# A second accumulation table for half of the expert pairs, read back midway, in a fused attention and mixture-of-experts kernel

## The chip, the cores and the metric

The kernel runs on one core of a Trainium2 chip. The metric is the device time of one execution in microseconds (us), as the median of several runs. The engines are named as the profile names them: PE (TensorE matmul, PEld its weight loads), DVE (VectorE), ACT (ScalarE), POOL (GpSimd) and SP (SyncE, which here only issues DMAs). A queue written SPq or POOLq is the engine's issuing of DMAs.

## The reference

The input x has 2 sequences of 1024 tokens with 256 values each, all float32. The block is

    x1  = layernorm(x + attention(x))
    out = layernorm(x1 + moe(x1))

- The attention has 16 heads of 128, RMS norm and rotary factors on queries and keys, scores capped by 50 * tanh(s / 50), a causal mask and softmax.
- The mixture of experts (MoE) routes each token to 6 of 32 experts, picked within 3 of 8 groups. Each expert takes its first 48 tokens at most. An expert computes silu(g) * u from one product (256 to 2 x 176) and a second product back to 256. Its rows are scaled by the token's weight and summed per token. A shared expert of 2 x 352 runs on every token and is added.

So behind the experts every token's row is a sum over up to six expert rows, and this sum is what the change touches.

## The kernel before

**Attention.** Eight pairs of heads, four steps each (two heads times two sequences) are run in a software pipeline: step s does the scores and softmax of its head while PE projects the queries and keys of step s+1. In each step the inverse RMS of the queries is written by SP to the table `rq_rows` in HBM in four small DMAs (line 344) and read back broadcast to all partitions into `rqB`, which is the tile `qsq` (line 346, function `rq_broadcast`). DVE scales the raw queries with it (line 1183) and splits them into a high and a low part, and then PE can compute scores.

**Start.** SP issues the first weights and x transposed, then x itself into `yacc` (line 337, semaphore `x_in`), in which the residual and the attention output add up. DVE waits for `x_in` right behind its splitting of x transposed, ahead of everything else of step 0. Then SP writes zeros from the tile `pacc` into the table `acc_rows` in nine DMAs (line 353) and into a strip of `x_rows` (line 354), and only then comes to the first `rq_broadcast`. POOL waits for the zeros before it starts step 0, as it will use `pacc` for the softmax sums from step 1 on.

**MoE.** After the routing POOL gathers the token rows of each pair of experts with an indirect DMA (`gather`, line 1054): 128 rows to a pair, 16 pairs. Four pairs form a group q with the semaphore `xg_in[q]`. PE turns the gathered rows (`slots_turned`, line 673, eight turns of a 128x512 tile, two to a group), DVE copies them to `xbT`. For pair p PE computes gate and up (`gate_up`, line 685), turns the activation (`turn_act`, line 696), and computes the down product (`expert_down`, line 706). The order of PE's work is written out by hand: gate_up(p+1), turn_act(p), then fillers, then expert_down(p). The fillers are the last piece of the shared expert's first product (`shared_up(11)`, line 594, dictionary `FILL_UP`) and twelve pieces of its second (`shared_down`, line 634, `FILL_DOWN`), which DVE adds into `yacc` (line 1436). `SLOT_TURNS` says behind which pairs the later groups are turned. Groups 0 and 1, eight gathered pairs, are turned before pair 0.

ACT scales the rows of a pair into one of four `ye` buffers (`expert_out`, line 907). POOL adds them to the rows of their tokens in `acc_rows` with an indirect DMA that accumulates (`scatter`, line 1060). The first expert of each pair has the upper half of `acc_rows` and the second the lower half, so that within one scatter no row is met twice; between scatters it may be, and so scatter p waits on POOL until scatter p-1 has landed (semaphore `added`). `expert_out(p)` waits until scatter p-4 has landed, as it reuses its buffer. Expert weights have eight buffers; SP loads those of pair p, 1.06 MB, as soon as the down product of pair p-8 is done (lines 383 and 384).

**End.** When all scatters have landed and PE has done the shared down products, SP reads `acc_rows` back into `accA` and `accB` (lines 401 and 402, sixteen DMAs). PE sums `yacc`, `accA` and `accB` in PSUM with identity matmuls (`add_rows`, line 638; the parts of `yacc` are done ahead), DVE takes the statistics, POOL the power, ACT normalises, and SP writes the output.

## Time and profile before

| | us |
|---|---|
| three runs | 1113.54, 1117.14, 1119.96 |
| median | 1117.14 |
| profiled execution | 1117.59 |
| its span, first to last instruction | 1115.9 |
| mean granted TensorE clock | 0.964 of full |

| engine | busy us | share of the span |
|---|---|---|
| PE | 1023.3 | 92% |
| PEld | 809.9 | 73% |
| DVE | 840.0 | 75% |
| ACT | 697.5 | 63% |
| POOL | 642.0 | 58% |

The busy shares are averages over stages with different limits: attention takes the first 900 us or so, routing and experts the rest. What bounds a stage is read from the chain that ended last and from the waits in that stage. The chain is followed back from the last instruction of the program, at each step to what released it. A DMA in it lasts from its issue to its landing. Granted clock 1.00 is 2.4 GHz for TensorE, 0.50 is 1.2 GHz.

### The profile page before, as it was taken

To read this page: it belongs to the slowest core of one execution; us is meant where nothing else is said; L and a number is where in the kernel's file an instruction comes from. 1 tells how busy PE (TensorE), PEld (TensorE's weight loads), DVE (VectorE), ACT (ScalarE), POOL (GpSimd) and SP (SyncE) were. 2 spreads that over 40 slices of the span, in tenths; PEclk is the share of its full clock that TensorE was granted. 3 is DMA by queue.
4 is the path that set the end of the run, shared out by engine and by line. 5 is a ranking of instruction groups with operands and counts; after the bars stand their busy time and mean duration, and the time that the engine had idled before them with its cause. 6 is when DMAs were issued, how large, how long until landed. Compare 5 with 4: busy or idle time off the path is not lost.

```text
span 1115.9 us, 17459 instructions
## 1 busy us (share of the span) xinstructions
PE 1023.3 (92%) x6048; PEld 809.9 (73%) x6048; DVE 840.0 (75%) x1376; ACT 697.5 (63%) x1159; POOL 642.0 (58%) x660
## 2 busy tenths in 40 slices
PE   4699999999999999999999999999999859889865
PEld 3478878887888788888878887888788746345432
DVE  3389898989898989888998889888988775613103
ACT  3377767777777777777777777777777723222212
POOL 0167666666676666666666666666667542353232
PEclk8899999999999999999999999999999978989888
DMA  9111011101100100010001000100000019539327
GB/s 337 46 39 33 24 36 40 33 30 39 30 20 29 39 30 20 30 39 29 20 29 39 30 20 29 40 29 20 20 20 20 20 30 289 129 101 253 74 29 231
DMA packets 47256, 66.77 MB, mean 60 GB/s; under 512 B 7904, under 2 KB 38592, under 8 KB 47168
## 3 DMA queue, kind: packets, MB, share of 16 engines
q1 hardware_dynamic: 43376, 60.65, 17.7%
q0 software_dynamic: 3072, 4.46, 2.3%
q8 instruction: 48, 0.79, 0.3%
q10 hardware_dynamic: 720, 0.54, 0.1%
q14 instruction: 40, 0.33, 0.1%
HBM read 54.35 MB, written 11.29 MB: 59 GB/s over the span
## 4 chain that ended last, share of the span: by engine, by line
PE 64%; DVE 14%; DMA 9%; issue 6%; POOL 3%; ACT 3%; SPq 1%; DVEq 0%; POOLq 0%; ACTq 0%
PE ps L417 19%; PE ps L418 18%; PE ps L419 17%; DMA acc_rows<-ye,acci 7%; DVE prob_lo L1098 7%; PE ps L451 5%; DVE qraw L1165 2%; PE ps L594 2%; POOL pacc L976 2%; PE ps L638 1%; DMA yacc<-in_x 1%; DVE qhat_lo L1098 1%; DVE qraw L1183 1%; DVE kT_lo L1098 1%; PE ps L604 1%
## 5 line engine op out<-in xcount | busy, mean ns | idle before, releaser
L1098 DVE TENSOR_TENSOR prob_lo<-praw,prob_hi 128x1024 fp32r<-128x1024 f32 (+7 forms) x256 | 304.6, 1213 | 1.7 <-ACT prob_hi L753 1.7
L959 POOL TENSOR_SCALAR_AFFINE_SELECT praw<-praw 128x128 f32<-128x128 f32 x256 | 120.7, 472 | 275.1 <-ACT praw L805 255.8
L976 POOL TENSOR_TENSOR pacc<-pacc,praw 128x768 f32<-128x768 f32 (+2 forms) x192 | 233.1, 1214 | 27.7
L799 ACT ACTIVATE praw<-ps,rk 128x1024 f32<-128x1024 f32 (+7 forms) x256 | 185.8, 740 | 64.3 <-PE ps L419 60.3
L753 ACT ACTIVATE prob_hi<-praw 128x1024 fp32r<-128x1024 f32 (+7 forms) x256 | 168.6, 685 | 1.3 <-POOL praw L959 1.3
L805 ACT ACTIVATE praw<-praw 128x1024 f32<-128x1024 f32 (+7 forms) x256 | 167.9, 683 | 0.0
L417 PE MATMUL ps<-qhat_hi,kT_hi 128*128 128x512 f32 (+3 forms) x384 | 135.1, 352 | 10.5 <-DVE qhat_lo L1098 10.1
L417 PE MATMUL ps<-prob_hi,vS_hi 128*128 128x512 f32 (+3 forms) x384 | 136.0, 354 | 6.0 <-DVE prob_lo L1098 6.0
L418 PE MATMUL ps<-prob_lo,vS_hi 128*128 128x512 f32 (+3 forms) x384 | 133.3, 347 | 0.0
L418 PE MATMUL ps<-qhat_lo,kT_hi 128*128 128x512 f32 (+3 forms) x384 | 133.0, 346 | 0.0
L419 PE MATMUL ps<-qhat_hi,kT_lo 128*128 128x512 f32 (+3 forms) x384 | 132.8, 346 | 0.0
L419 PE MATMUL ps<-prob_hi,vS_lo 128*128 128x512 f32 (+3 forms) x384 | 132.5, 345 | 0.0
L417 PE MATMUL ps<-xT_hi,wqk_hi 128*128 128x512 f32 x256 | 103.3, 404 | 23.8 <-DVE xT_lo L1098 11.9
L1210 DVE SCALAR_TENSOR_TENSOR yacc<-ps,rsum,yacc 128x256 f32<-128x256 f32 x256 | 111.5, 477 | 6.7 <-PE ps L419 5.8
L418 PE MATMUL ps<-xT_lo,wqk_hi 128*128 128x512 f32 x256 | 102.2, 399 | 0.0
L419 PE MATMUL ps<-xT_hi,wqk_lo 128*128 128x512 f32 x256 | 101.8, 397 | 0.0
L417 PEld LDWEIGHTS ps<-qhat_hi,kT_hi 128*128 128x128 f32 x384 | 72.8, 190 | 30.8 <-issue 12.8
L417 PEld LDWEIGHTS ps<-prob_hi,vS_hi 128*128 128x128 f32 x384 | 72.6, 189 | 17.6 <-DVE prob_lo L1098 12.1
L774 ACT ACTIVATE ksq<-ps 128x512 f32<-128x512 f32 x64 | 38.3, 599 | 65.8 <-PE ps L419 65.8
L419 PEld LDWEIGHTS ps<-qhat_hi,kT_lo 128*128 128x128 f32 x384 | 72.7, 189 | 8.4
L419 PEld LDWEIGHTS ps<-prob_hi,vS_lo 128*128 128x128 f32 x384 | 72.4, 189 | 8.2
L418 PEld LDWEIGHTS ps<-qhat_lo,kT_hi 128*128 128x128 f32 x384 | 73.0, 190 | 6.0
(161 smaller groups left out, 2255.6 us busy)
## 6 DMA issues: line engine op xcount, KB each, us to landing
qsq<-rq_rows SPq DMA_DIRECT2D x32, 512.0 KB, 4.0
wgu<-in_wgu SPq DMA_DIRECT2D x16, 704.0 KB
wd<-in_wd SPq DMA_DIRECT2D x16, 352.0 KB
wraw<-in_wqkv SPq DMA_DIRECT2D x16, 256.0 KB, 4.5
acc_rows<-pacc SPq DMA_DIRECT2D x8, 512.0 KB, 10.5
wvraw<-in_wqkv SPq DMA_DIRECT2D x16, 128.0 KB, 2.7
woraw<-in_wo SPq DMA_DIRECT2D x16, 128.0 KB, 4.1
yacc<-in_x SPq DMA_DIRECT2D x1, 2048.0 KB, 13.8
```

Source lines behind the costliest of these rows:

```text
L417: mm(out_, left[0], right[0], start=start, stop=False)
L418: mm(out_, left[0], right[1], start=False, stop=False)
L419: return mm(out_, left[1], right[0], start=False, stop=stop)
L451: last = mm(ps[32 * g:32 * g + 32, bank_no, c0:c0 + 32 * TT].rearrange("p (j r) -> p j r", r=32), ones[:, :], by_strip[:, g], start=True, ...
L753: return nc.scalar.activation(dst, src, ACT.Copy)
L774: nc.scalar.activation(ksq[:, cols], bank, ACT.Square).then_inc(ksq_done, 1)
L799: nc.scalar.activation(praw[:, raw_at(b, j)], buf[:, P * j:T], ACT.Tanh, scale=rk[:, b, j:j + 1]).then_inc(tanh_done, 1)
L805: nc.scalar.activation(tile, tile, ACT.Exp, scale=CAP).then_inc(exp_done, 1)
L959: nc.gpsimd.affine_select(out=diag, in_=diag, compare_op=ALU.is_ge, fill=0.0, base=0, pattern=[[1, P]], channel_multiplier=-1).then_inc(ma ...
L976: nc.gpsimd.tensor_tensor(pacc[:, P * j:T], before, raw, ALU.add).then_inc(pacc_done, 1)
L1098: v.tensor_tensor(dst, x_, hi.bitcast(F32), ALU.subtract).then_inc(done, 1)
L1210: last = v.scalar_tensor_tensor(y, ps[:, bank_no, D * i:D * i + D], rsum[:, k, 2 * u + i:2 * u + i + 1], y, ALU.mult, ALU.add)
```

## The change

- A second table, `acc2_rows`, of the size of `acc_rows`. Pairs 1, 3, 5 and 7 scatter into it (`SIDE`), the other twelve into `acc_rows` (`MAIN`). Each table has its own semaphore, and a scatter waits only for the one before it on its own table.
- When the four side scatters have landed, SP reads `acc2_rows` back in eight DMAs of 512 KB into `accA`, the last four of them each after an add that frees its place. DVE adds them to `yacc` in eight additions of 128x1024, two each behind pairs 11, 12, 14 and 15 (`SIDE_ADDS`). SP waits for all eight before it reads `acc_rows` as before, and PE before it sums `yacc`.
- Both tables are zeroed. The zero writes stand behind the first `rq_broadcast` on SP, and POOL waits for them ahead of step 1, no more ahead of step 0.
- DVE waits for x ahead of step 1.
- Only group 0 is turned before pair 0. Groups 1, 2 and 3 are turned behind pairs 1, 4 and 7, where groups 2 and 3 were behind pairs 2 and 5. The last `shared_up` moves from pair 0 to pair 1, the first `shared_down` from pair 1 to pair 0. Gathers 10 to 15 are issued two at a time behind scatters 0, 1 and 2.

```diff
-FILL_UP = {0: 11}
-FILL_DOWN = {p: p - 1 for p in range(1, 13)}
+FILL_UP = {1: 11}
+FILL_DOWN = {0: 0} | {p: p - 1 for p in range(2, 13)}
-SLOT_TURNS = {2: 2, 5: 3}
+SLOT_TURNS = {1: 1, 4: 2, 7: 3}
+SIDE = [p for p in range(WR) if p % 2]
+MAIN = [p for p in range(PAIRS) if p not in SIDE]
+SIDE_ADDS = {11: (0, 1), 12: (2, 3), 14: (4, 5), 15: (6, 7)}
...
+        def written(engine, p):
+            if p in SIDE:
+                engine.wait_ge(side_added, 16 * (SIDE.index(p) + 1))
+            else:
+                engine.wait_ge(added, 16 * (MAIN.index(p) + 1))
...
+            rq_broadcast(0, 0)
             sp.wait_ge(zeros_set, 1)
             zero = pacc[:, :]
-            rows = acc_d.rearrange("(p r) d -> p (r d)", p=P)
-            for c0 in range(0, 2 * ACCR // P * D, T):
+            for table in (acc_d, acc2_d):
+                rows = table.rearrange("(p r) d -> p (r d)", p=P)
+                for c0 in range(0, 2 * ACCR // P * D, T):
...
-            rq_broadcast(0, 0)
...
-            sp.wait_ge(added, 16 * PAIRS)
+            sp.wait_ge(side_added, 16 * len(SIDE))
+            sp.wait_ge(gu_read, SHARED_UNITS)
+            for n in range(8):
+                if n >= 4:
+                    sp.wait_ge(side_done, n - 3)
+                four = slice(4 * (n % 4), 4 * (n % 4) + 4)
+                sp.dma_start(accA[:, four, :], side_v[n // 4][:, four, :]).then_inc(side_in[n], 16)
+            sp.wait_ge(side_done, 8)
+            sp.wait_ge(added, 16 * len(MAIN))
             sp.wait_ge(sd_done, NT)
...
+                if n == SHARED_FOURTH:
+                    pe.wait_ge(sd_added, 1)
...
-                if i == 0:
+                if i == 1:
                     pe.wait_ge(gu_read, SHARED_UNITS)
...
-                if n >= 2:
-                    pe.wait_ge(xbt_read, n - 1 if n < 2 * KC else n)
+                if n >= KC:
+                    pe.wait_ge(xbt_read, n)
...
-            for n in range(2 * KC):
+            for n in range(KC):
                 slots_turned(n)
             gate_up(0)
...
             pe.wait_ge(sd_added, ADDED)
+            pe.wait_ge(side_done, 8)
...
                 if p >= 4:
-                    act.wait_ge(added, 16 * (p - 3))
+                    written(act, p - 4)
...
-            pool.wait_ge(zeros_out, 16 * ((2 * ACCR // P * D + T - 1) // T + 1))
-            for q in range(STEPS):
+            step(Step(0, 0, "first"))
+            pool.wait_ge(zeros_out, 16 * (2 * ((2 * ACCR // P * D + T - 1) // T) + 1))
+            for q in range(1, STEPS):
                 step(Step(0, q, "first"))
...
             def scatter(p):
                 pool.wait_ge(ey_evac, p + 1)
-                if p:
-                    pool.wait_ge(added, 16 * p)
-                nc.gpsimd.indirect_dma_start(acc_d, bass.IndirectOffsetOnAxis(ap=acci[:, p:p + 1], axis=0), ye[:, p % 4, :], None,
-                                             compute_op=ALU.add).then_inc(added, 16)
+                row = bass.IndirectOffsetOnAxis(ap=acci[:, p:p + 1], axis=0)
+                if p in SIDE:
+                    if SIDE.index(p):
+                        pool.wait_ge(side_added, 16 * SIDE.index(p))
+                    nc.gpsimd.indirect_dma_start(acc2_d, row, ye[:, p % 4, :], None, compute_op=ALU.add).then_inc(side_added, 16)
+                else:
+                    if MAIN.index(p):
+                        pool.wait_ge(added, 16 * MAIN.index(p))
+                    nc.gpsimd.indirect_dma_start(acc_d, row, ye[:, p % 4, :], None, compute_op=ALU.add).then_inc(added, 16)
...
-            for p in range(8, 12):
+            late = list(range(8, PAIRS))
+            for p in late[0:2]:
                 gather(p)
             for p in range(PAIRS):
-                if p in FILL_UP:
-                    shared_product(FILL_UP[p])
                 scatter(p)
                 if p == 1:
-                    for g in range(12, PAIRS):
-                        gather(g)
+                    shared_product(FILL_UP[p])
+                for g in late[2 * p + 2:2 * p + 4]:
+                    gather(g)
...
             split_x(1)
-            dve.wait_ge(x_in, 16)
...
-            for q in range(STEPS):
+            step(Step(0, 0, "first"))
+            rows_in()
+            for q in range(1, STEPS):
                 step(Step(0, q, "first"))
...
+            def add_side(n, shared):
+
+                dve.wait_ge(side_in[n], 16)
+                dve.wait_ge(sd_added, shared)
+                if n >= 4:
+                    dve.wait_ge(side_done, n - 3)
+                four = slice(4 * (n % 4), 4 * (n % 4) + 4)
+                v.tensor_tensor(yacc[:, four, :], yacc[:, four, :], accA[:, four, :], ALU.add).then_inc(side_done, 1)
...
-            for n in range(2 * KC):
+            for n in range(KC):
                 slots_turned(n)
...
                 if p in FILL_DOWN:
                     add_shared(FILL_DOWN[p])
+                for n in SIDE_ADDS.get(p, ()):
+                    add_side(n, min(p, ADDED))
```

## Rows read from the trace of the kernel before

**Rows 1.** Page of the profile: the chain that ended last, shares of the span by line.

```profile
PE ps L417 19%; PE ps L418 18%; PE ps L419 17%; DMA acc_rows<-ye,acci 7%; DVE prob_lo L1098 7%; PE ps L451 5%; DVE qraw L1165 2%; PE ps L594 2%; POOL pacc L976 2%; PE ps L638 1%; DMA yacc<-in_x 1%; DVE qhat_lo L1098 1%; DVE qraw L1183 1%; DVE kT_lo L1098 1%; PE ps L604 1%
```

**Rows 2.** Chain of waits, 0 to 70 us: start us, duration us, engine or DMA and line.

```profile
5.78 13.78 DMA yacc<-in_x
19.59 0.70 DVE qraw L1165
...
34.17 3.77 DMA qsq<-rq_rows
...
61.73 1.20 DVE qraw L1183
```

**Rows 3.** Timelines of DVE and PE, start: us, duration, operation [idle before it <- what ended it].

```profile
14.97 2.29 DVE L1098 TENSOR_TENSOR xT_lo<-praw,xT_hi 128x2048 fp32r<-128x2048 f32 x1 [0.38 <-ACT xT_hi L753]
...
20.33 0.79 PE L417 MATMUL ps<-xT_hi,wqk_hi 128*128 128x512 f32 x1 [3.78 <-DVE qraw L1165]
```

**Rows 4.** Timeline, SP queue, 0 to 140 us.

```profile
6.34 11.43 SPq L353 DMA_DIRECT2D acc_rows<-pacc  x9
...
54.34 1.30 SPq L344 DMA_DIRECT2D rq_rows<-sqT  x4
```

**Rows 5.** Windows: PE, PEld, DVE, ACT, POOL busy (count), then PEclk, DMA share, GB/s.

```profile
20.00:25.00 5.00, 4.67 (x11) 3.70 (x12) 1.39 (x3) 1.09 (x2) 0.00 (x0) 0.50 1.03 419
1020.00:1025.00 5.00, 4.59 (x30) 2.86 (x32) 2.13 (x5) 0.32 (x1) 0.00 (x0) 1.00 1.00 243
```

**Rows 6.** Timeline, PE, 957 to 1040 us.

```profile
980.52 1.04 PE L673 MATMUL ps<-ident,xg 128*128 128x128 f32 x8
986.69 1.97 PE L673 MATMUL ps<-ident,xg 128*128 128x128 f32 x8 [5.13 <-DMA xg<-x_rows,toki]
988.59 4.12 PE L685 MATMUL ps<-wgu,xbT 128*64 128x352 f32 x16
...
992.89 3.60 PE L594 MATMUL ps<-x1T,wsgu 128*96 128x512 f32 x8
...
997.33 1.36 PE L685 MATMUL ps<-wgu,xbT 128*64 128x352 f32 x8
...
1001.18 1.36 PE L685 MATMUL ps<-wgu,xbT 128*64 128x352 f32 x8
...
1006.57 0.66 PE L673 MATMUL ps<-ident,xg 128*128 128x128 f32 x4 [0.78 <-DVE xbT L1419]
```

**Rows 7.** Chain of waits, 860 to 1116 us.

```profile
1006.65 8.49 DMA acc_rows<-ye,acci
...
1025.76 9.13 DMA acc_rows<-ye,acci
...
1046.65 3.80 DMA acc_rows<-ye,acci
...
1087.25 3.87 DMA acc_rows<-ye,acci
...
1091.55 3.03 DMA accB<-acc_rows
```

**Rows 8.** Timeline, POOL, 910 to 1116 us.

```profile
986.21 0.98 POOL L1054 DMA_INDIRECT xg<-x_rows,toki  x1 [0.16 <-issue]
...
1008.52 1.01 POOL L1054 DMA_INDIRECT xg<-x_rows,toki  x1 [0.30 <-issue]
```

**Rows 9.** DMA issues, 1005 to 1016 us: what, queue, count, median us to landing.

```profile
xg<-x_rows,toki POOLq DMA_INDIRECT x4, 6.3
```

**Rows 10.** Timeline, PE, 1040 to 1116 us.

```profile
1061.24 0.42 PE L696 MATMUL ps<-ident,actE 128*88 128x128 f32 x2 [1.37 <-DVE actE L1425]
...
1065.74 0.66 PE L696 MATMUL ps<-ident,actE 128*88 128x128 f32 x2 [2.48 <-DVE actE L1425]
...
1068.81 3.78 PE L638 MATMUL ps<-yacc,ident 128*128 128x512 f32 x4
...
1094.62 2.07 PE L638 MATMUL ps<-accA,ident 128*128 128x512 f32 x2 [11.10 <-DMA accB<-acc_rows]
```

More of the change, by code:

```diff
@@ L139, in block_kernel @@
     acc_d = nc.dram_tensor("acc_rows", (2 * ACCR, D), F32, kind="Internal").ap()
+    acc2_d = nc.dram_tensor("acc2_rows", (2 * ACCR, D), F32, kind="Internal").ap()
     ctx = ExitStack()
@@ L301, in block_kernel @@
         et_done, et_read = sem("et_done"), sem("et_read")
-        ey_done, ey_evac, added = sem("ey_done"), sem("ey_evac"), sem("added")
+        ey_done, ey_evac, added, side_added = sem("ey_done"), sem("ey_evac"), sem("added"), sem("side_added")
+        side_in, side_done = [sem(f"side_in{n}") for n in range(8)], sem("side_done")
         acc_in = [sem(f"acc_in{k}") for k in range(NT // 2)]
         sum_done, var2, rln2, nmr_done, norm_done, out_done = sem("sum_done"), sem("var2"), sem("rln2"), sem("nmr_done"), sem("norm_done"), sem("out_done")
+        def written(engine, p):
[3 more added lines that the diff above has]
+                engine.wait_ge(added, 16 * (MAIN.index(p) + 1))
         def sum_place(i):
@@ L316, in block_kernel @@
         accB_v = acc_d[ACCR:ACCR + N, :].rearrange("(i p) d -> p i d", p=P)
+        side_v = [acc2_d[ACCR * u:ACCR * u + N, :].rearrange("(i p) d -> p i d", p=P) for u in range(2)]
         out_v = out.rearrange("(i p) d -> p i d", p=P)
@@ L346, in rq_broadcast @@
                 sp.dma_start(rqB[:, :], rq_d[b:b + 1, :].to_broadcast([P, T])).then_inc(rqB_in, 16)
+            rq_broadcast(0, 0)
             sp.wait_ge(zeros_set, 1)
             zero = pacc[:, :]
-            rows = acc_d.rearrange("(p r) d -> p (r d)", p=P)
-            for c0 in range(0, 2 * ACCR // P * D, T):
-                cn = min(T, 2 * ACCR // P * D - c0)
-                sp.dma_start(rows[:, c0:c0 + cn], zero[:, 0:cn]).then_inc(zeros_out, 16)
+            for table in (acc_d, acc2_d):
+                rows = table.rearrange("(p r) d -> p (r d)", p=P)
+                for c0 in range(0, 2 * ACCR // P * D, T):
+                    cn = min(T, 2 * ACCR // P * D - c0)
+                    sp.dma_start(rows[:, c0:c0 + cn], zero[:, 0:cn]).then_inc(zeros_out, 16)
             sp.dma_start(x1_d[N:ACCR, :], zero[:, 0:XD]).then_inc(zeros_out, 16)
-            rq_broadcast(0, 0)
             next_wqkv = wqkv_d[2:H].rearrange("(n e) p m c d -> n e p m c d", e=2)
@@ L669, in slots_turned @@
                     pe.wait_ge(xg_in[q], 16 * 4)
-                if n >= 2:
-                    pe.wait_ge(xbt_read, n - 1 if n < 2 * KC else n)
+                if n >= KC:
+                    pe.wait_ge(xbt_read, n)
                 for r in range(4):
-                    last = nc.tensor.transpose(ps[:, n % 2 if n < 2 * KC else 1, P * r:P * r + P], xg[:, 4 * q + r, P * c:P * c + P], ident[:, :])
+                    last = nc.tensor.transpose(ps[:, n % 2 if n < KC else 1, P * r:P * r + P], xg[:, 4 * q + r, P * c:P * c + P], ident[:, :])
                 last.then_inc(xbt_done, 1)
@@ L691, in turn_act @@
                 if p == 0:
-                    pe.wait_ge(xbt_read, 2 * KC)
+                    pe.wait_ge(xbt_read, KC)
                 else:
@@ L1202, in tile, with rows_in @@
                 lo_of(prob[1][:, AT[j]:AT[j] + n], praw[:, raw_at(b, j)], prob[0][:, AT[j]:AT[j] + n], plo_done)
+            def rows_in():
+                dve.wait_ge(x_in, 16)
             def out_projected(b, k, u, step, count, bank_no):
@@ L1418, in slots_turned @@
                 dve.wait_ge(xbt_done, n + 1)
-                v.tensor_copy(xbT[:, c, 512 * q:512 * q + 512], ps[:, n % 2 if n < 2 * KC else 1, :]).then_inc(xbt_read, 1)
+                v.tensor_copy(xbT[:, c, 512 * q:512 * q + 512], ps[:, n % 2 if n < KC else 1, :]).then_inc(xbt_read, 1)
             def product(p):
```

## The prediction, made before the changed kernel was run

> **What bounds the kernel now.** I read the page first, then the chain of waits at both ends, then the timelines of the engines in those stretches. The change touches the first step of the attention and everything behind the routing; the 900 us between keep their work, so what is gained or lost at the start is only carried through them. The page gives the scatter-adds into `acc_rows` 7% of the chain that ended last [rows 1]. The chain of waits shows how: from 1006.65 to 1091.1 it is one scatter-add after another, because each waits on POOL for the one before to land. While expert weights are loading one takes 8.5 to 9.1 us, with idle DMA engines 3.8 to 3.9; from the one at 1046.65 to the last at 1087.25 are nine steps of 4.51, so 0.7 us lie between a landing and the next start [rows 7]. PE could go faster: a pair costs it 3.85 us (997.33 to 1001.18) [rows 6], and at 1083.5 it has done all its other work and idles 11.1 us for the rows read back [rows 10]. From pair 1 on the scatter chain sets the time.
>
> Two waits ahead of that chain matter. The first pair can't start until eight gathers have landed: PE idles 5.13 us, turns the second four tiles in 1.97, and then needs 4.12 us for the sixteen gate-and-up matmuls of two pairs, where eight take 1.36 later [rows 6]. And at the start DVE stands from 17.26 (14.97 + 2.29 [rows 3]) to 19.59 for the load of x into `yacc` [rows 2], which nothing needs before step 1; PE idles 3.78 us meanwhile [rows 3] and comes back at the lower of its two clocks (granted 0.50, 1.2 GHz, from 20 to 25 us [rows 5]).
>
> **Part 1, the start.** The wait for x leaves step 0. DVE copies the first queries at 17.3 instead of 19.6: 2.3 us. PE then pauses 1.5 us instead of 3.8. The two key projections behind it are 12 matmuls, before at half clock (11 in 4.67 us [rows 5]); at full clock they would end 2.4 us earlier. That the clock holds is an estimate from the pair stage: after a pause of 1.37 us two small matmuls took 0.42 us, after one of 2.48 us they took 0.66 [rows 10]. Together the chain to the first `rq` broadcast comes 4.7 us earlier; bounds 2.3 and 4.9.
>
> The zero writes move behind that broadcast and double: nineteen DMAs, 9.06 MB, from about 29.9 (34.17 + 0.4 less 4.7 [rows 2]). At the 419 GB/s of [rows 5] they take 21.6 us, to 51.5. The DMA engines were free then. POOL's wait for them stands before the first use of `pacc` in step 1, which comes near the end of step 0, where DVE scales the next queries at 61.73 [rows 2], now 57.0: hidden by some 5 us. But SP's queue is full when the second `rq` broadcast comes. Its source was ready at 54.3 [rows 4], now at 49.6; its small writes get behind the zeros' tail and 0.26 MB of `wvraw` and land near 53.5, and the broadcast itself, 3.8 us [rows 2], near 57.5, where DVE wants it at 57.0. I charge 0.7 us, between 0 (the small writes slip through) and 5 (the zeros go at 0.33 MB/us). SP's issuing is no limit: nine zero DMAs took 11.43 us to issue with other loads ahead [rows 4]. Net of part 1: **-4.0 us**, with ends -4.9 and +1.
>
> **Part 2, the first pair.** PE turns tiles 0 and 1 by 981.56 (980.52 + 1.04 [rows 6]); DVE's copy keeps it some 0.9 us, as the 0.78 at 1006.57, and at 982.45 pair 0 may start. Gone are the rest of the wait for the gathers, the second turning and, as the pause is short, the half clock: two products in 2.4 instead of 4.1. The last shared product (3.60 busy, 3.43 until the next can start [rows 6]) moves to pair 1, and a shared down product takes its place; one of these and the down product are what is left of a pair's 3.85 after 1.2 for gate-and-up and 0.35 for the turn: 2.3 together. So 982.45 + 2.4 + 0.35 + 2.3 = 987.5 for the end of pair 0, where it was 997.4: 9.9 us earlier. POOL's gather 8 was issued at 986.21, and 8 and 9 with 1.3 each end at 988.8 [rows 8], just clear for scatter 0. Pair 1 takes 1.2 + 0.35 + 3.43 + 1.0 = 6.0 us and ends at 993.5; the two turnings with the copy between cost 2.0, so pair 2 ends at 999.4, then 3.85 each with 2.0 more behind pairs 4 and 7: 1003.2, 1007.1, 1012.9, 1016.8, 1020.6 and 1026.5 (pair 8). The other gathers are out behind scatter 2 and late for nothing.
>
> **Part 3, the side table.** Scatters 0, 2, 4, 6 and 8 to 15 are one chain, 1, 3, 5, 7 another; POOL issues both in order. Behind a pair's end I put 1.6 us for ACT's two copies and the issue. Under load a scatter's step is 9.1 + 0.7 = 9.8 us, and two may now fly at once. Even: 0 at 989, 2 at 1001, 4 at 1011, 6 at 1020.5. Odd: 1 at 995, 3 at 1005, 5 at 1015, 7 at 1024.5, landing before 1030 as the loads stop. These, eight of 1.06 MB at the 243 GB/s of [rows 5], start 10 us earlier too and are over near 1026. How much two in flight slow each other no row shows directly. The nearest: the scatter of 1006.65 took 8.49 us though four gathers followed it on the same queue from 1008.52 on [rows 7, 8], no longer than the 9.13 at 1025.76 with nothing behind it, and these gathers, in flight together, landed 6.3 us after their issue each [rows 9]. So I take no slowdown; the other end is that they take turns.
>
> By the Trainium skill (DMA: Bandwidth & Descriptors, Queues, rings and completion order) each DMA engine goes round between its queues and drains a packet of one before it changes to the next. Both scatters stand in the one queue of POOL, so while SP's loads keep theirs full the second would win no share of its own. By that rule the sum would be that of rival A.
>
> Scatter 8 waits for 6 alone and issues when its rows are ready, at 1028.3. Before it was issued at 1055.6 (1087.25 less seven steps of 4.52 [rows 7]): 27.3 us later. The readback gives part of it back. When scatter 7 has landed SP reads both side halves, 4.2 MB; at 0.33 MB/us (between the 419 and the 243 GB/s of [rows 5]) that loads the DMA engines for 12.7 us between 1030 and 1047. Scatters 8 to 10 then need 5.6 to 7.5 us instead of 3.8: I charge 8, between 0 and 12 (two and a half at the loaded price). The last lands at 1091.1 - 27.3 + 8 = 1071.8: **-19 us** for parts 2 and 3.
>
> The eight adds of 128x1024 cost DVE some 1.15 us each (half of the 2.29 for 128x2048 in [rows 3]), 9 us in all, behind pairs 11, 12, 14 and 15. DVE comes to pair 11 near 1037, after the first side rows are in (1033), and has added all by 1054; what stands behind them, the turn of pair 12, is 7 us ahead of its scatter. PE's sums now also wait for the adds: they ran from 1068.81 to 1083.5 [rows 10] and now run from 1054 to 1069, still ahead of 1071.8, cover of 3 us. ACT only reads another semaphore. Behind the last scatter all is as before, 24.8 us to the end of the span, the accumulated rows read back in 3.0 us [rows 7] and PE cold as before.
>
> **Sum.** The profiled execution took 1117.59 us, its span 1115.9, so 1.7 lie around it; it stands 0.45 above the median of 1117.14. 1117.6 - 4 - 19 = 1094.6, against the median 0.4 less: **about 1094.3 us**.
>
> **Rivals.**
> *A, two scatters in flight take turns.* If under load each doubles the other's time, the first eight last until 1040, the readback runs from 1042 to 1056, and the last lands near 1081: 9.5 us gained in place of 19, total 1104. For it: the loaded price is itself a time in queues. Against it: the gathers beside the scatter of 1006.65. Chance 0.2.
> *B, the zeros block the start.* They run at the 243 GB/s of the weight loads, 37 us, to 67; the second `rq` broadcast lands near 72, 15 us behind its need. Part 1 becomes +10, total 1108.5. Against it: the 419 GB/s of [rows 5] were largely these writes. Chance 0.05.
> *C, slower: the side readback becomes the end.* From the last side scatter to the last add lie four loads, four more that wait for adds, and the work of pairs 14 and 15, some 24 us; then PE's 15 us of sums, which must end before SP may read `acc_rows`. To be 5.6 us slower than before SP must start at 1100.7 (1091.1 + 4 + 5.6), so scatter 7 would have to land after 1061, 32 us behind my date. With steps of 17 us in both chains that happens: total 1123 or more. No row asks such a price. Chance 0.02.
> *D, little comes through:* loads, readback and adds eat what the two chains give, 1111.6 to 1122.7. Chance 0.03.
>
> **Numbers.** Forecast 0.7, A 0.2, B 0.05, C 0.02, D 0.03. About 0.5%, 5.6 us, is what a measurement can tell from no change: faster 0.95, same 0.03, slower 0.02. The forecast's own bounds are 1087 (start -4.9, readback 3 instead of 8, scatters at 7 us under load) and 1100 (start 0, readback 10); the range goes on to A: 1087 to 1105.
>
> **What would show it.** DVE's first `qraw` copy near 17.3 and PEclk at 1.0 between 18 and 22; the zeros between 30 and 52, the broadcast of step 1 landing near 57; pair 0's down product 10 us earlier behind the turning of tile 0; side scatters overlapping main ones at 9 us each, not 18; scatter 8 some 27 us earlier, scatter 15 some 19. I am wrong if a loaded scatter with a partner takes over 12 us, if DVE idles at the first side add, or if PE's sums end after the last scatter lands.

## The result, and the profile after

The changed kernel takes 1101.19 us (median of 4 runs, 1099.12 to 1103.33), the kernel before beside it 1117.33 (1113.54 to 1119.96): a ratio of 0.9863, 95% interval 0.9836 to 0.9889, so 16 us less where 23 were forecast. The profiled execution took 1103.33 us, its span 1101.6 where it was 1115.9.

The pair stage first: the chain of waits of the changed kernel from 985 us on (start us, duration us, what), where [rows 7] stood.

```profile
1033.65 3.82 DMA acc_rows<-ye,acci
...
1038.20 7.41 DMA acc_rows<-ye,acci
...
1046.34 4.25 DMA acc_rows<-ye,acci
...
1056.20 5.82 DMA acc_rows<-ye,acci
...
1071.84 3.87 DMA acc_rows<-ye,acci
...
1079.32 16.47 PE ps L661 x32
```

Scatter 8 at 1033.65 is the first link; ahead of it the chain is PE's pairs, no scatter. Of the eight scatters in the chain four take the quiet 3.8 us (two of them are left out here); the four from 1038.20 to 1056.20 take more (the one left out among them, of 1051.32, took 4.15). The timeline of PE, where [rows 6] stood:

```profile
985.63 1.04 PE L696 MATMUL ps<-ident,xg 128*128 128x128 f32 x8
987.66 2.59 PE L708 MATMUL ps<-wgu,xbT 128*64 128x352 f32 x16 [0.99 <-DVE xbT L1453]
...
991.83 1.08 PE L729 MATMUL ps<-wd,actT 88*64 88x256 f32 x8
```

PE waits 0.99 us for DVE's copy in place of the gathers, and pair 0's down product ends 7.3 us behind the turning of tile 0. The scatters 0 to 7, main and side, by tile, issued between 985 and 1032 us:

```profile
L1091 POOL DMA_INDIRECT acc_rows<-ye,acci x4: 1560/1611/1638, 994.2 to 1023.8; - x4
L1087 POOL DMA_INDIRECT acc_rows<-ye,acci x4: 1557/1592/1623, 1000.2 to 1028.4; - x4
...
DMA to landing us min/median/max: 6.5/7.1/7.7
```

L1087 is the side table, L1091 the main one. Eight scatters start in 34 us. Each is in flight together with the next for 0.4 to 4.2 us; the one issued at 1010.69 had a partner for 6.7 of its 7.4 us. None lands later than 7.7 us after its issue; one at a time they took 8.5 to 9.1 [rows 7].

So the stage did what it was meant to. From the turning of tile 0 to the last landing it took 1091.12 - 980.52 = 110.6 us and takes 1075.71 - 985.63 = 90.1: **20.5 us less** (forecast 19). But tile 0 is turned at 985.63 in place of 980.52: the stage starts **5.1 us later**, where 4.0 earlier was forecast. That came from the start. SP's queue, 28 to 90 us, where [rows 4] stood:

```profile
30.18 0.35 SPq L358 DMA_DIRECT2D qsq<-rq_rows  x1
30.57 21.16 SPq L367 DMA_DIRECT2D acc_rows<-pacc  x18
...
55.09 1.35 SPq L356 DMA_DIRECT2D rq_rows<-sqT  x4
57.65 0.34 SPq L358 DMA_DIRECT2D qsq<-rq_rows  x1
...
86.14 1.30 SPq L356 DMA_DIRECT2D rq_rows<-sqT  x4
```

The last row is the writes of the third broadcast, which in the kernel before were these:

```profile
82.31 1.30 SPq L344 DMA_DIRECT2D rq_rows<-sqT  x4
```

The first `rq` broadcast is issued at 30.18 (34.17 before [rows 2]): the 4 us are there. Then SP spends 21.16 us on issuing eighteen zero DMAs, 1.2 us each. That is about as long as one takes to move (0.52 MB at 418 GB/s is 1.25 us), so SP is held back, and the second broadcast goes out at 57.65. The zeros are also in flight longer than SP is issuing them: those issued from 48 us on land 5.0 to 6.3 us after their issue, so the last ones behind 55 us. What the DMA engines moved, in slices of 1 us from 25 to 65 us:

```profile
GB/s 0 0 0 1 3 0 152 233 332 410 434 410 426 418 418 430 410 426 404 424 406 410 422 426 414 422 414 418 420 383 264 132 13 57 283 270 365 82 0 0
```

DVE at 14 to 25 us and at 60 to 70 us:

```profile
17.46 1.28 DVE L1194 COPY qraw<-ps 128x512 f32<-128x512 f32 x2
...
61.68 2.21 DVE L1212 SCALAR_TENSOR_TENSOR qraw<-qraw,gcur,qsq 128x1024 f32<-128x1024 f32 x1 [3.10 <-DMA qsq<-rq_rows]
63.92 2.18 DVE L1138 CAST qhat_hi<-qraw 128x1024 fp32r<-128x1024 f32 x1
66.14 2.44 DVE L1128 TENSOR_TENSOR qhat_lo<-qraw,qhat_hi 128x1024 fp32r<-128x1024 f32 x1
```

The first copy came at 17.46 (19.59 before). At 61.68 DVE has waited 3.10 us, and its three operations take 6.8 us where the same three at 34.63 took 1.28, 0.69 and 1.22. The POOL timeline beside them:

```profile
60.70 2.11 POOL L1000 TENSOR_TENSOR pacc<-praw 128x896 f32<-128x896 f32 x1 [0.15 <-POOL pacc L996]
62.95 9.38 POOL L1000 TENSOR_TENSOR pacc<-pacc,praw 128x768 f32<-128x768 f32 x6
```

POOL is adding up `pacc` all that time. The whole balance: +5.1 at the start of the stage, -20.5 in it, and +1.1 behind it (PE's last sums took 16.47 us, 15.44 before): 14.3 us, which are the spans' 1115.9 - 1101.6. The +1.1 is not shown to come from the change: in the two versions of the kernel before that follow below the same sums took 16.03 and 15.86 us.

Of the 5.1 us, 3.8 are there at the third `rq` broadcast, whose writes SP issues at 86.14 us where it was 82.31, and are carried through the attention. The other 1.3 I put down to PE's clock: from 935 to 945 us it was granted 0.50, the 1.2 GHz level (the PEclk column of the windows, as in [rows 5]), where it had 0.71 and 0.95 before. At the start, from 15 to 25 us, it was at full speed. Changed kernel:

```profile
15.00:25.00 10.00, 7.21 (x45) 4.96 (x43) 5.56 (x7) 4.07 (x8) 0.00 (x0) 1.00 0.33 104
...
935.00:940.00 5.00, 5.00 (x25) 5.00 (x25) 0.00 (x0) 3.99 (x6) 0.08 (x1) 0.50 0.98 257
940.00:945.00 5.00, 5.00 (x18) 4.03 (x19) 1.39 (x3) 0.00 (x0) 1.18 (x1) 0.50 0.97 310
```

and before:

```profile
935.00:940.00 5.00, 5.00 (x23) 3.15 (x23) 2.68 (x19) 1.30 (x3) 1.27 (x1) 0.71 0.97 269
940.00:945.00 5.00, 5.00 (x12) 2.02 (x11) 4.85 (x36) 2.37 (x3) 1.26 (x1) 0.95 1.04 264
```

From the third broadcast's writes to the turning of tile 0 it is 899.5 us here and 898.2 before. Of the versions below with the same start, the one that also had 0.50 from 935 to 945 us (the two-table run) took 899.6, the others, at higher clocks, 897.7 to 898.5. So a difference of one or two microseconds between two profiles need not be the edit's.

### The profile page after: what moved, and what is told of

Its sections match the earlier page's. It is cut to its first block, busy times and chain, and to the rows that moved or that the text cites. A ratio compares the mean times of both kernels' runs of the same rounds, so it can differ in the third digit from the quotient of the medians.

```text
span 1101.6 us, 17494 instructions
## 1 busy us (share of the span) xinstructions
PE 1019.9 (93%) x6048; PEld 810.3 (74%) x6048; DVE 848.3 (77%) x1384; ACT 698.1 (63%) x1159; POOL 643.0 (58%) x660
## 3 DMA queue, kind: packets, MB, share of 16 engines
q0 software_dynamic: 3072, 4.46, 2.2%
## 4 chain that ended last, share of the span: by engine, by line
PE 69%; DVE 15%; issue 5%; DMA 5%; SPq 2%; POOL 2%; ACT 2%; DVEq 0%; ACTq 0%; POOLq 0%
PE ps L438 19%; PE ps L439 18%; PE ps L440 18%; DVE prob_lo L1128 6%; PE ps L472 5%; DMA acc_rows<-ye,acci 3%; PE ps L617 3%; SPq L367 2%; DVE qraw L1194 2%; POOL pacc L1000 2%; PE ps L661 1%; PE ps L708 1%; DVE qraw L1212 1%; DVE kT_lo L1128 1%; PE ps L657 1%
## 5 line engine op out<-in xcount | busy, mean ns | idle before, releaser
L798 ACT ACTIVATE ksq<-ps 128x512 f32<-128x512 f32 x64 | 38.4, 599 | 60.6 <-PE ps L440 60.6
```

Source lines behind the costliest of these rows:

```text
L798: nc.scalar.activation(ksq[:, cols], bank, ACT.Square).then_inc(ksq_done, 1)
```

## The experiments

**The start alone.** The kernel before with part 1 of the change; once with one table's zeros, once with both.

```diff
 e1_start_one_table and e2_start_two_tables, against the kernel before
+            rq_broadcast(0, 0)
             sp.wait_ge(zeros_set, 1)
 (e2)        for table in (acc_d, acc2_d):
...
-            rq_broadcast(0, 0)
...
-            dve.wait_ge(x_in, 16)
...
-            for q in range(STEPS):
+            step(Step(0, 0, "first"))
+            dve.wait_ge(x_in, 16)
+            for q in range(1, STEPS):
```

> The kernel before with part 1 of the change alone and one table: x is waited for behind step 0, the first rq broadcast stands ahead of the zeros, POOL waits for the zeros behind step 0, but only the nine zero DMAs of acc_rows and the strip are written. Theory Q (SP stands at a full queue: in the changed kernel eighteen zero DMAs are issued 1.2 us apart from 30.6 on, so SP is free for the second broadcast only at 55.1 and not at 51.2): nine are issued by about 42, the second broadcast goes out on time, DVE scales the queries of step 1 at about 58.5 instead of 61.7, and the time is 3 to 4 us below before: 1113.5. Rival X (moving the wait for x or the order on SP costs by itself, whatever the number of zeros): as slow as with two tables, 1119 to 1121.

> The same as the run with one table, but both tables are zeroed, so part 1 of the change in full and nothing of the rest; the second table is not used. Theory Q: the second broadcast lands at 61.7, 3 us late, DVE's three operations behind it run into POOL's additions into pacc and take 6.8 us instead of 3.2, and everything behind is 3.8 us later than before: 1121, so 7 us above the run with one table. Rival X: the same time as the run with one table. If the sum of parts holds, this run less 20 us is the changed kernel.

Measured: one table 1112.65 us (ratio 0.9965, 0.9946 to 0.9984), two tables 1119.29 (1.0036, 1.002 to 1.0053), the kernel before 1116.06. Both are within 2 us of theory Q, and rival X falls. The second table's zeros alone cost 6.6 us and turn the gain of the start into a loss. SP's queue and DVE with one table:

```profile
29.63 9.69 SPq L354 DMA_DIRECT2D acc_rows<-pacc  x9
...
56.71 1.28 DVE L1183 SCALAR_TENSOR_TENSOR qraw<-qraw,gcur,qsq 128x1024 f32<-128x1024 f32 x1
```

and with two:

```profile
30.27 21.17 SPq L357 DMA_DIRECT2D acc_rows<-pacc  x18
...
61.38 2.47 DVE L1186 SCALAR_TENSOR_TENSOR qraw<-qraw,gcur,qsq 128x1024 f32<-128x1024 f32 x1 [2.83 <-DMA qsq<-rq_rows]
```

Nine zero DMAs take 1.08 us each to issue as well, but are over before the second `rq` broadcast is ready (its writes go out at 49.39); eighteen are not. The rows with two tables are the changed kernel's over again: the start's loss needs nothing of the pair stage. What these two runs don't separate is whether the broadcast's writes are late because SP can't issue them or because they stand in its queue behind zeros that are still moving at 55 us; with more zeros both come together.

**The collision at 61 us.** The changed kernel, in which POOL holds step 1's first `pacc` work until DVE has made `qhat_lo`.

```diff
 e4_pool_held
+                    if st.first and st.q == 1:
+                        pool.wait_ge(qlo_done, 2)
```

> The changed kernel with one wait more: in step 1 POOL starts its additions into pacc only when DVE has split the queries of step 1. Theory P (the second half of the loss is that the late scaling and splitting, 2.21, 2.18 and 2.44 us instead of 1.28, 0.69 and 1.22, run beside POOL's additions and hold each other up at SBUF): the three take 3.2 us again, scores of step 1 start 3.6 us earlier, and of this 2 to 3.6 us stay, as POOL's additions end about as late as before the change: 1098.5. Rival Z (they were slow for another reason, such as the DMA just landing): the three stay at 6.8 us and the time is the changed kernel's or worse.

Measured: 1099.13 us (0.9853, 0.9822 to 0.9884), 2.1 us below the changed kernel; the intervals of the two ratios overlap, so the trace must say it. DVE, and POOL behind it:

```profile
60.55 1.28 DVE L1214 SCALAR_TENSOR_TENSOR qraw<-qraw,gcur,qsq 128x1024 f32<-128x1024 f32 x1 [3.64 <-DMA qsq<-rq_rows]
61.88 0.69 DVE L1140 CAST qhat_hi<-qraw 128x1024 fp32r<-128x1024 f32 x1
62.60 1.23 DVE L1130 TENSOR_TENSOR qhat_lo<-qraw,qhat_hi 128x1024 fp32r<-128x1024 f32 x1
...
64.03 0.29 POOL L996 COPY pacc<-praw 128x128 f32<-128x128 f32 x1 [5.39 <-DVE qhat_lo L1130]
```

The wait for the broadcast stays (3.64), the three operations are back at 3.2 us. So the wait comes with the zeros, and the slow DVE is POOL's additions beside it. Tile 0 is turned at 978.30, 7.3 us earlier than in the changed kernel; of these the third broadcast shows 5.9 (80.21 against 86.14), of which 1.0 was there at the first one (29.21 against 30.18), ahead of anything that the edit touches. The rest goes with PE's clock, granted 0.66 and 1.00 from 935 to 945 us and not 0.50. But the pair stage took 94.6 us in place of 90.1, and ate most of it: see below.

**Zeros that hold nobody.** The changed kernel with a zero tile of its own; after the first `rq` broadcasts each step's broadcast is followed by one zero DMA, and POOL waits for the zeros only before its scatters.

```diff
 e3_spread
+        zsrc = sb("zsrc", [P, 256])
...
+            def zeros_piece():
+                if pieces:
+                    dst, src = pieces.pop(0)
+                    sp.dma_start(dst, src).then_inc(zeros_out, 16)
...
-            pool.wait_ge(zeros_out, 16 * (2 * ((2 * ACCR // P * D + T - 1) // T) + 1))
...
+            pool.wait_ge(zeros_out, 16 * ZERO_PIECES)
```

> The changed kernel with the zeros taken from a 128x256 tile of their own and written one DMA at a time behind each of the following rq broadcasts, eighteen zero DMAs and two for the strip over the first five pairs of heads; POOL waits for them only ahead of the gathers. Theory Q: start as with one table, -3.5 us against before instead of +3.8, so 7 us below the changed kernel: 1094. Rival Y (what was lost at the start was lost to DMA bandwidth or to the longer table as such, and 512 KB of zeros a step disturb the broadcasts anyway): within 2 us of the changed kernel, 1099 to 1102.

Measured: 1097.11 us (0.983, 0.9796 to 0.9863), and 1097.15 (0.9841, 0.981 to 0.9873) when it was run once more beside the gated versions below. That lies between theory Q (1094) and rival Y (1099 to 1102). The start did more than theory Q asked: the writes of the second `rq` broadcast go out at 49.27, those of the third at 77.22, 5.1 us ahead of the kernel before, each zero DMA takes 0.44 us to issue, and DVE takes 1.28 us at 56.59. Tile 0 is turned at 976.71, 8.9 us before the changed kernel's. Only 4.1 of them arrive in the medians, too few for the intervals of the two ratios to part: the pair stage takes 94.7 us here too (94.5 in the second profile, whose two slow issues take 2.24 and 4.46 us). The timelines of POOL and DVE in it:

```profile
1038.63 2.44 POOL L1105 DMA_INDIRECT acc_rows<-ye,acci  x1 [6.36 <-DMA acc_rows<-ye,acci]
1046.41 4.37 POOL L1105 DMA_INDIRECT acc_rows<-ye,acci  x1 [5.34 <-DMA acc_rows<-ye,acci]
...
1038.41 2.36 DVE L1489 TENSOR_TENSOR yacc<-yacc,accA 128x1024 f32<-128x1024 f32 x2
1044.39 2.35 DVE L1489 TENSOR_TENSOR yacc<-yacc,accA 128x1024 f32<-128x1024 f32 x2
1047.00 2.35 DVE L1489 TENSOR_TENSOR yacc<-yacc,accA 128x1024 f32<-128x1024 f32 x2
```

Two scatters are issued in 2.44 and 4.37 us in place of 1.56, and both stand beside DVE's additions of the side rows. In the changed kernel the scatter of 1056.20 took 3.50 us to issue beside the additions of 1055.92, and the one of 1046.34 was issued 1.0 us ahead of the additions of 1047.33 and escaped. Counted from the turning of tile 0, the additions of pair 12 stand at +61.7 in both kernels and scatter 10 at +60.7 there, +61.9 here: a shift of 1.2 us decides.

The second run of this version (1093.95 to 1104.49 us in six executions) shows what the clock alone can do. Its profile is of the slowest execution, 1104.49 us. Its third broadcast goes out 0.3 us later than in the first profile, but its tile 0 is turned 6.1 us later, at 982.78: from 930 to 945 us PE was granted 0.50 there and 1.00 in the first. The same matmuls, first profile and second:

```profile
928.81 3.66 PE L642 MATMUL ps<-gwT,x1T 128*128 128x32 f32 x32
932.86 6.88 PE L642 MATMUL ps<-gwT,x1T 128*128 128x32 f32 x32
```

**A gate for DVE's additions.** The spread version, in which POOL counts its scatters and DVE's additions behind pairs 11, 12, 14 and 15 wait for scatters 9, 10, 11 and 12.

```diff
 e8_gated, against e3_spread
+ADD_BEHIND = {11: 9, 12: 10, 14: 11, 15: 12}
...
+                pool.sem_inc(issued, 1)
...
+                if p in ADD_BEHIND:
+                    dve.wait_ge(issued, ADD_BEHIND[p] + 1)
```

> The version with the spread zeros, and VectorE's side adds of pairs 11, 12, 14 and 15 now start only behind the issue of scatter 9, 10, 11 and 12. Theory (an add of 128x1024 on VectorE keeps GpSimd from issuing the scatter beside it: 1.56 us became 2.4 and 4.4 in the spread version): every scatter is issued in some 1.6 us, the stage from the turn of tile 0 to the last landing takes 90 to 91 us instead of 94.7, the time is 1097.1 - 4 = 1093. Rival (the adds don't hold the issues, or what they cost comes back as TensorE's sums, which wait for the last add): within 1.5 us of the spread version, 1095.6 to 1098.6.

> The spread version once more on the chip of the gated ones, for the difference: 1097 again, within 1.5 us.

Measured: 1093.62 us (1092.13 to 1094.57; 0.9806, 0.9779 to 0.9832) against 1097.15 of the spread version beside it, 3.5 us less, with intervals that overlap. The stage took 90.8 us. POOL's timeline, and DVE's additions behind pairs 12, 14 and 15:

```profile
1036.58 1.56 POOL L1107 DMA_INDIRECT acc_rows<-ye,acci  x1 [6.34 <-DMA acc_rows<-ye,acci]
1042.41 1.56 POOL L1107 DMA_INDIRECT acc_rows<-ye,acci  x1 [4.28 <-DMA acc_rows<-ye,acci]
1046.85 2.49 POOL L1107 DMA_INDIRECT acc_rows<-ye,acci  x1 [2.87 <-DMA acc_rows<-ye,acci]
...
1037.68 2.36 DVE L1492 TENSOR_TENSOR yacc<-yacc,accA 128x1024 f32<-128x1024 f32 x2
1043.67 2.35 DVE L1492 TENSOR_TENSOR yacc<-yacc,accA 128x1024 f32<-128x1024 f32 x2
1046.67 2.36 DVE L1492 TENSOR_TENSOR yacc<-yacc,accA 128x1024 f32<-128x1024 f32 x2 [0.33 <-POOLq L1108]
```

Scatters 10 and 11 are issued in 1.56 us and follow at 5.83 and 4.44 (7.78 and 7.63 in the spread version); scatter 12 is now hit instead. But the gate is not what spared 10 and 11. Only the additions of 1046.67 waited for POOL. Those of pair 12 stand at +61.7 behind the turning of tile 0, where they stood without the gate; it is scatter 10 that comes at +60.6 and not at +61.9. The reason lies ahead of every gated addition: scatter 8 landed after 3.97 us and not 5.24. So scatters 10 and 11 start 1.1 and 1.3 us ahead of the additions and escape, as scatter 10 did in the changed kernel. Where the gate did act it leaked: POOL's counter moves 0.2 us ahead of the scatter behind which it stands in the program, so DVE's additions start with the scatter.

Of the stage's 3.9 us 1.3 are scatter 8's landing, and 2.6 follow from it (step by step 1.95 and 3.19 gained, 2.53 given back at scatter 12). So the theory's time and stage came out, but the trace doesn't show them as the gate's work, and what the gate is worth stays open. The rival's first half, that the additions don't hold the issues, falls all the same. In the profiles of this document eleven issues of scatters 10 to 13 took 2.05 to 4.53 us, all beside such additions; in those without additions (before, one table, two tables, and the two below without a readback) none of these took over 1.56. And the gate, where it acted, put the additions 0.2 us ahead of a scatter, once here and twice in the last run below: 2.49 us each time. This version also beats the changed kernel, by 7.6 us in the medians and 6.4 by the ratios, whose intervals just don't meet (0.9832 and 0.9836 are their nearest ends).

**The side table alone.** The changed kernel with all sixteen scatters in one table, no readback and no additions (the second table is still zeroed).

```diff
 e5_no_side
-SIDE = [p for p in range(WR) if p % 2]
+SIDE = []
...
-SIDE_ADDS = {11: (0, 1), 12: (2, 3), 14: (4, 5), 15: (6, 7)}
+SIDE_ADDS = {}
...
-            sp.wait_ge(side_added, 16 * len(SIDE))
...
-                sp.dma_start(accA[:, four, :], side_v[n // 4][:, four, :]).then_inc(side_in[n], 16)
...
-            pe.wait_ge(side_done, 8)
```

> The changed kernel without the side table's use: all sixteen scatters in one chain on acc_rows, no readback midway, no adds, everything else as changed (the second table is still zeroed). Theory S (in the changed kernel PE sets the pace up to scatter 8, as two chains keep up with it; with one chain of 7.5 to 9 us steps under load the scatters fall behind PE by pair 4): the last scatter lands 95 to 98 us behind the turning of tile 0, where it is 90.1 with the side table, so 1107, and the side table is worth some 6 us, the earlier first pair 13 to 15. Rival A of the prediction (two in flight take turns, so one chain is as good): within 1.5 us of the changed kernel or faster, as the readback and the adds are gone.

Measured: 1108.96 us (0.9943, 0.9923 to 0.9964), stage 98.5 us, and rival A falls. The side table is worth 1109.0 - 1101.2 = 7.8 us, its readback already paid. In the chain of waits scatter 5 is still slow, and the first quiet scatter is the seventh, scatter 6:

```profile
1030.71 5.05 DMA acc_rows<-ye,acci
...
1036.49 3.79 DMA acc_rows<-ye,acci
```

**The first pair alone.** The changed kernel with the side table, but the first pair, its turnings and gathers as before.

```diff
 e7_turns8
-SLOT_TURNS = {1: 1, 4: 2, 7: 3}
+SLOT_TURNS = {2: 2, 5: 3}
...
-            for n in range(KC):
+            for n in range(2 * KC):
                 slots_turned(n)
...
```

> The changed kernel with the pair stage's order of before: two groups of gathered rows turned ahead of pair 0, the last shared product in pair 0, gathers as before; the side table stays. Theory S (PE sets the pace up to scatter 8): pair 0 ends 10 us later, pair 1 has 2.1 us less to do and one turning less stands between, so scatter 8 goes out some 6 us later and the time is 1107. Rival (the scatter chains set it throughout and have slack for a late start): 1102 or less.

Measured: 1111.74 us (0.9937, 0.9914 to 0.996), 4.7 above what was expected; stage 100.8. So the new first pair is worth 1111.7 - 1101.2 = 10.5 us. PE:

```profile
990.03 1.97 PE L694 MATMUL ps<-ident,xg 128*128 128x128 f32 x8 [5.11 <-DMA xg<-x_rows,toki]
```

The wait for the gathers is back. Taken out singly, the two parts lengthen the stage by 8.4 and 10.7 us, together 19.1 of the 20.5 that it gained: nearly additive, where the two forecast times, 1107 each, had put only 6 us on either.

**The readback's price.** The changed kernel with the side table written, but neither read back nor added: the output lacks the contributions of pairs 1, 3, 5 and 7.

```diff
 e6_no_readback
-SIDE_ADDS = {11: (0, 1), 12: (2, 3), 14: (4, 5), 15: (6, 7)}
+SIDE_ADDS = {}
...
-                sp.dma_start(accA[:, four, :], side_v[n // 4][:, four, :]).then_inc(side_in[n], 16)
...
-            pe.wait_ge(side_done, 8)
```

> The changed kernel with the side table written but neither read back nor added, so the output lacks the rows of pairs 1, 3, 5 and 7. My term for the readback was 8 us. The trace of the changed kernel has scatter 9 at 7.41 us, 10 at 4.25, 11 at 4.15 and 12 at 5.82, where the quiet ones take 3.8: 6.4 us in all. Theory R (all of that is the readback's DMAs and, for scatter 12, a DVE add that holds POOL's issue, 3.50 us instead of 1.56): all are at 3.8, 1095. Rival (the rest of the weight loads slows them): scatter 9 stays above 6 us and the time falls by 3 us or less.

Measured: 1096.27 us (0.9816, 0.9787 to 0.9845), 4.9 below the changed kernel (the intervals overlap a little), and the stage is 4.9 shorter, 85.1 us. Scatters 8 and 9:

```profile
1031.45 4.95 DMA acc_rows<-ye,acci
...
1037.14 3.66 DMA acc_rows<-ye,acci
```

From scatter 9 on all are near the quiet price, with 4.37 us for scatter 12 as the highest. Scatter 8 took 4.95 us here, 1.1 more than in the changed kernel, so the 4.9 us are rather too low for the readback and the additions.

**One more pair on the side.** As the gated version, with pair 9 in the side table and the additions behind pairs 12 to 15.

```diff
 e9_side_of_five, against e8_gated
-SIDE = [p for p in range(WR) if p % 2]
-ADD_BEHIND = {11: 9, 12: 10, 14: 11, 15: 12}
+SIDE = [1, 3, 5, 7, 9]
+ADD_BEHIND = {12: 10, 13: 11, 14: 12, 15: 13}
```

> As the gated version, with pair 9's scatter on the side chain too (five side, eleven main), so that the main chain has one step of some 4.5 us less, while the side readback starts one scatter later. Theory (the main chain sets the end all the way): pair 9 and pair 8 may fly together, the last landing comes 2 to 4 us earlier, time 1091 (2 below the gated version). Rival (from there TensorE's sums, which wait for the last side add, or the readback beside later scatters set the end): same as the gated version within 1 us, or slower by up to 3, and TensorE then has no idle time ahead of its last turns.

Measured: 1092.57 us (1089.98 to 1094.94; 0.9795, 0.9767 to 0.9824), 1.1 below the gated version: not to be told from it. The last scatter lands 90.0 us behind the turning of tile 0, 0.8 earlier than in the gated version, where the theory had 2 to 4. POOL and PE show why there is no more:

```profile
1031.99 1.56 POOL L1107 DMA_INDIRECT acc_rows<-ye,acci  x1 [2.29 <-ACT ye L948]
...
1046.66 2.49 POOL L1107 DMA_INDIRECT acc_rows<-ye,acci  x1 [4.61 <-ACT ye L948]
1052.08 2.49 POOL L1107 DMA_INDIRECT acc_rows<-ye,acci  x1 [2.93 <-DMA acc_rows<-ye,acci]
...
1069.93 1.13 PE L678 MATMUL ps<-accA,ident 128*128 128x512 f32 x2 [0.54 <-DMA accB<-acc_rows]
```

Scatter 10, issued at 1031.99 as SP begins the readback at 1031.96, lands only after 7.8 us, and the leaking gate lets DVE's additions start with scatters 12 and 13. PE idles 0.54 us ahead of its last sums, where it idled 6.59 in the gated version, and it is still the rows read back that it waits for: its own sums, which the rival named, are not the bound yet, but 0.5 us away from it. What the rows show is the rival's other half, the readback beside later scatters.

## Why the prediction was right and wrong

The time fell in the range and the sign was right; 6.9 us too much was promised. The profiled execution, 2.1 us slower than the median, misses by more, 8.7 us: 7.8 at the third broadcast (part 1), 1.3 behind it with the clock, 1.1 in the tail, less 1.5 that the pair stage gained over its forecast. So nearly all of it is part 1.

**Part 1, the steps that failed: "SP's issuing is no limit" and the zeros' end at 51.5.** The first was read from nine DMAs issued in 11.43 us with loads ahead [rows 4]. That row was itself the limit: 1.27 us each, where SP issues an unhindered DMA in 0.35 to 0.5. Eighteen of them take 21.16. The prediction knew that the queue would be full and that the broadcast's writes would stand behind the zeros' tail, and had them land near 53.5. But SP issued the last zeros at 51.78, and the DMA engines were at their full rate until about 55: the rate was as forecast, but it was reached only at 34 us (233 GB/s from 32 to 33 us), and 0.5 MB of the first broadcast moved with the zeros. The writes' source was ready at 51.2; they were *issued* at 55.09. So its 57.5 for the landing became 61.66, and a wait of 0.5 us one of 3.10. How much of the 4 us an SP that is never held would have saved, with the zeros still moving, no run shows. The term behind it was not in the sum at all: DVE's three operations then fell beside POOL's additions, 3.6 us. Charged were 0.7 us; against the forecast -4.0 the third broadcast stood at +3.8, a miss of 7.8. The two-table run shows a loss of 3.2 us in the time with nothing of the pair stage changed, the one-table run the gain of 3.4 that this part has without the second table; there the third broadcast's writes came 5.0 us earlier (forecast without the charge 4.7).

The rest of part 1 held: first copy at 17.46 (17.3), PE at full clock, granted 1.00 from 15 to 25 us, first broadcast 4.0 us earlier (4.7). The range's end for part 1, +1, was too near. Rival B, that the zeros block the start, priced the case at +10 with a slower transfer rate as its cause; the rate was as forecast (418 GB/s from 34 to 51 us).

**Part 2** held: PE's pause 0.99 (0.9), pair 0's down product 7.3 us behind the turning of tile 0 (7.0).

**Part 3** held in size. Scatter 8 is issued 48.0 us behind the turning of tile 0 (forecast 47.8, before 75.1). The four slow scatters behind it take 6.4 us more than 3.8 each, where 8 was charged; the run without readback, whose own scatter 8 was 1.1 us slower, puts the whole of it at 4.9. The last lands at +90.1 (91.3). What the prediction missed inside that term is its kind: it charged DMA traffic, but a part is DVE holding POOL's issue. It was luck that this cost little: by the accident of its timing one scatter was hit here; in two versions with an earlier start two were, and the stage was 4.6 us longer; in the gated version, which started as early, it was one again.

**Rival A fell**: 7.1 us (the median) for a loaded scatter, and 7.4 for the one that had a partner nearly all the time, far from the 12 that would have spoken for it. The rule from the Trainium skill beside it (DMA: Bandwidth & Descriptors, Queues, rings and completion order) was read as: a second scatter on POOL's queue wins nothing while SP's loads keep theirs full. The measured 7.1 us decide against this reading of it; nothing here shows how the packets were in fact shared out. **Rival C fell**: the side rows were there before DVE came to them (its first addition, at 1043.48, has no idle time before it), and PE's sums ended 2.3 us ahead of the last landing (3 forecast).

**The tail**, "behind the last scatter all is as before", was 1.1 us too low: PE's last 32 matmuls took 16.47 us in place of 15.44. As said, executions of the kernel before with another start took 15.86 and 16.03, so this is no fault of the step.

Of the slow scatters, 9 is the readback's traffic, at least in its first part: it was issued in the usual 1.56 us and had been in flight for 5.3 us, more than a quiet one takes, when DVE's first side addition began (1043.48). In the five-pair run the one issued with the readback was slow too (7.8 us), whatever its number.

What stays open: why PE's clock fell at 935 us in some executions and not in others, which cost 6 us between two executions of the same kernel; why scatter 8 landed after 3.82 us in one profile and 5.65 in another, which decides what the later ones fall beside; and what the gate is worth, which was not tried on a counter that moves only behind the issue.

## What to carry to other kernels

A row in which one engine issues equal DMAs at well over its usual time (here 1.1 to 1.3 us in place of 0.4) shows an engine that is held at its queue: more DMAs there cost it their transfer time, and the next small, urgent one behind them waits for all. Spread bulk writes that nobody needs soon between the urgent ones; here that brought the third broadcast 8.9 us forward, of which 4.1 arrived. Look at what a late operation falls beside: wide VectorE operations and GpSimd's additions or indirect DMAs, harmless apart, cost 0.5 to 3 us each when they meet. And before a gate gets the credit, look in the trace whether anything waited at it.

## What the runs showed of the hardware

- DVE operations on 128x1024 beside POOL's additions took 2.21, 2.18 and 2.44 us in place of 1.28, 0.69 and 1.22; POOL's six additions of 128x768 took 9.38 us in place of 8.04. With POOL held back DVE's were at 1.28, 0.69 and 1.23 again. By the Trainium skill (SBUF — State Buffer, SBUF: two separate sides) VectorE and GpSimd share one pair of ports, which one of them locks for a whole instruction while the other is blocked, where the VectorE operation uses both of its ports or has two inputs in SBUF and GpSimd's reads SBUF; these rows agree in kind, and the page gives no time for such a pair of operations.
- An indirect DMA with addition, issued in 1.56 us on POOL, took 2.05 to 3.50 us to issue beside one pair of DVE additions of 128x1024, and 4.37 to 4.53 when it met the end of one pair and the whole of the next. All eleven of these began while the additions were already running; those that had begun 0.4 to 1.3 us ahead of the additions (in the changed kernel, the gated, the five-pair and the first-pair version) kept their 1.56.
- In the changed kernel the loaded ones, on POOL's queue beside full weight loads and partly two in flight, landed 6.5 to 7.7 us after their issue, in the other traces with a side table that show the landings 6.1 to 9.9. One at a time they took 6.8 to 9.1 in the kernel before and 4.5 to 8.8 in the version without the side table: about as long.
- SP issues a DMA in 0.35 to 0.5 us, a 512 KB zero write that stands alone in 0.44, and the same size in 1.1 to 1.3 us each when nine or eighteen follow one another.
- A counter that POOL raises behind an indirect DMA in program order released DVE 0.2 us ahead of that DMA's record, three times out of three.
- The same kernel, with PE granted 1.00 and 0.50 from 930 to 945 us, turned tile 0 at 976.71 and 982.78 us.
